# A four-layer preactivation network: the order tables of all engines are replaced

## The reference

```python
x = x + L0(_gn(x))   # three gates over (C,W), (H,C), (H,W): max and mean pool, 7x7 convolution,
                     # batch norm, sigmoid; the three are mixed by a softmax over pooled channels
x = x + L1(_gn(x))   # 3x3 convolution, 256 to 256; its weight is a softmax mix of the weight and
                     # of its circulant projections with blocks of 2, 4, 8 and 16
x = x + L2(_gn(x))   # squeeze and excitation on the mean of the wavelet's low band
x = x + L3(_gn(x))   # shifted window attention: 8x8 windows, 8 heads, bias table, mask
```

## Time and profile before

| | us |
|---|---|
| median of 3 runs | 2878.24 (2876.93 to 2885.32) |
| profiled execution | 2871.03 |
| its span, first to last instruction | 2869.2 |
| mean granted TensorE clock | 0.938 of full |
| PE busy | 2368.1 |
| DVE busy | 2303.8 |
| ACT busy | 1654.8 |
| POOL busy | 1390.7 |

### The profile page before, as it was taken

The page is one execution under the profiler, slowest core; times in us unless marked ns, Lnnn a source line. Parts: engine busy times, 40 slices in busy tenths (PEclk is TensorE's granted clock), DMA queues, the critical chain, the costliest instruction groups (busy, mean ns, idle before and its releaser), DMA issues. The chain is left out here.

```text
span 2869.2 us, 68252 instructions
## 1 busy us (share of the span) xinstructions
PE 2368.1 (83%) x27252; PEld 1337.8 (47%) x27252; DVE 2303.8 (80%) x4579; ACT 1654.8 (58%) x4200; POOL 1390.7 (48%) x1132
## 2 busy tenths in 40 slices
PE   0376828899798988899798988899798988899788
PEld 0232315444554545444554545444454545444555
DVE  7877866879888797979878797979878797978665
ACT  0322137754866568664866558664866558664665
POOL 2413561355724564355724565354824565354454
PEclk9968968999899989999899999999999999999999
DMA  5400310015010241004110241004110141001111
GB/s 147 121 1 16 122 42 24 31 38 170 16 46 23 82 133 31 31 31 148 45 46 24 76 139 32 31 31 139 55 46 24 62 145 39 31 30 45 61 52 47
DMA packets 90337, 176.13 MB, mean 61 GB/s; under 512 B 37526, under 2 KB 50470, under 8 KB 80422
## 3 DMA queue, kind: packets, MB, share of 16 engines
...
## 5 line engine op out<-in xcount | busy, mean ns | idle before, releaser
L2021 PE MATMUL F<-g_raw,cw_hi 128*128 128x512 f16 x2304 | 700.0, 386 | 28.1 <-DVE ytj L1454 10.9
L879 POOL TENSOR_TENSOR xs<-xs,rec 128x512 f32<-128x512 f32 x256 | 282.0, 1102 | 731.4 <-DVE rec L1796 728.5
L1158 ACT ACTIVATE xs<-xs,mx 128x64 f32<-128x64 f32 x1792 | 447.4, 336 | 131.4 <-DVE mx L1791 131.4
L2021 PE MATMUL F<-g_raw,cw_lo 128*128 128x512 f16 x1152 | 443.6, 385 | 0.0
L2021 PEld LDWEIGHTS F<-g_raw,cw_hi 128*128 128x128 f16 x2304 | 222.6, 99 | 296.4 <-issue 19.6
L1780 DVE TENSOR_TENSOR xs<-SP,bias 128x512 f32<-128x512 f32 (+2 forms) x384 | 181.8, 501 | 120.2 <-PE SP L2112 118.8
L864 POOL TENSOR_TENSOR tmp<-X,uw 128x512 f32<-128x512 f32 x128 | 171.5, 1351 | 179.1 <-DVE X L1636 114.3
L1795 DVE TENSOR_REDUCE sums<-xs 128x8 f32<-128x512 f32 x256 | 172.9, 675 | 95.1 <-ACT xs L1158 69.2
L2080 PE MATMUL QP<-tok_hi,qkv_hi 128*128 128x512 f16 x470 | 182.8, 389 | 51.9 <-ACT qq L1139 28.9
L1369 DVE SCALAR_TENSOR_TENSOR g_raw<-l0c,gn,g_raw 128x512 f16<-128x512 f32 x192 | 171.2, 934 | 50.0 <-ACT g_raw L1016 35.2
L2140 PE MATMUL O<-prt,vv 64*32 64x64 f32 x8192 | 175.0, 228 | 32.1 <-ACT prt L1165 28.3
...
## 6 DMA issues: line engine op xcount, KB each, us to landing
scratch_x<-X SPq DMA_DIRECT2D x32, 1024.0 KB, 7.4
...
X<-in_x SPq DMA_DIRECT2D x25, 1024.0 KB, 5.5
...
l0c<-in_x SPq DMA_DIRECT2D x7, 1024.0 KB, 5.6
...
```

The costliest lines, as they stand in the source:

```text
L879: G.tensor_tensor(keyed(sc[:, u % 4, :]), keyed(sc[:, u % 4, :]), rec[:, u % 4, :].unsqueeze(2).to_broadcast([P, 8, TOK]), ALU.mult).then_ ...
L1158: last = S.activation(keys, keys, ACT.Exp, bias=mx[:, u % 4, i:i + 1])
L2021: last = T.matmul(F[:, n % 2, :], wgt[:, ci, C3 * comp + dx, P * co:P * co + P], win[which], start=(ci == 0 and dx == 0 and j == 0), stop= ...
```

## The change

The four tables get new contents for all five engines: `FIRST`, `TURN` and `LAST_ROWS` in full, and in `AHEAD` seven entries: SP `S` 1 to 2, `Z` 2, `F` 1 and `G` 1 new; ACT `Q` 4 to 5 and `K` 1 to 2; DVE `S` 2 to 3; PE `S` 1 new. Each stream keeps its items and their order, and no other line of the program changes. Cut to what is spoken of below:

```diff
--- before.py
+++ after.py
@@ -50,96 +50,95 @@
 FIRST = {
-    "SP": {"reduce0": "Y", "reduce11": "Y", "hwgate": "Y", "band1": "Z", "band2": "YF", "hwmean3": "Z",
-        "conv10.0": "G", "conv13.0": "F", "conv14.0": "F", "conv15.0": "Z", "conv22.1": "F", "convend": "ZL"},
-    "POOL": {"load": "RR", "norm0a": "Y", "norm0b": "RY", "reduce0": "R", "reduce4": "R", "reduce5": "RR",
-        "reduce7": "R", "reduce9": "R", "reduce12": "RRRR", "reduce13": "R", "reduce14": "R", "zpool": "R",
-        "hwgate": "RRRRR", "hwrows": "R", "band0": "R", "band1": "R", "band2": "R", "band3": "R", "hwmean4": "R",
-        "hwmean5": "R", "lift2": "D", "conv0.1": "Y", "conv2.0": "D", "conv3.0": "DD", "conv7.1": "D",
-        "conv8.0": "W", "conv8.1": "D", "conv9.0": "W", "conv11.1": "WW", "conv13.1": "W", "conv14.0": "W",
-        "conv15.0": "W", "conv16.1": "W", "conv19.0": "W", "conv20.0": "W", "conv21.1": "W", "conv23.0": "WWWWW",
-        "convend": "RRRRERRRRRRRRRRRRRRERRRRRRRRRR"},
...
-    "DVE": {"load": "YYCCUCCCCCCCCCUCCUYYYYYYYYCYCYCY", "norm0a": "Y", "norm0b": "YYUU", "norm0c": "YYYYYYYYYYY",
-        "reduce1": "UU", "reduce2": "Y", "reduce3": "U", "reduce4": "UU", "reduce5": "U", "reduce6": "UU",
-        "reduce8": "U", "reduce10": "UU", "hwrows": "Y", "band0": "Y", "band1": "Y", "hwmean2": "Y",
-        "hwmean3": "Y", "logits": "Y", "mix": "Y", "mixturn": "Y", "gate12": "Y", "gate14": "Y", "gate15": "Y",
-        "norm1c": "Y", "conv1.0": "B", "conv2.0": "Y", "conv5.0": "B", "conv6.0": "B", "conv6.1": "BJ",
-        "conv7.1": "J", "conv8.1": "BJB", "conv10.0": "BBVVY", "conv11.0": "V", "conv11.1": "Y", "conv12.1": "V",
-        "conv13.0": "JVYJ", "conv13.1": "JB", "conv14.1": "B", "conv15.0": "VB", "conv15.1": "BVV",
-        "conv16.1": "BV", "conv17.0": "VYVV", "conv18.0": "VVJYJ", "conv19.1": "VC", "conv20.1": "VJCVY",
-        "conv21.0": "VCV", "conv21.1": "C", "conv22.0": "CVC", "conv22.1": "CV", "conv23.0": "V",
-        "conv23.1": "VUY", "convend": "VJJJVVVVVVVVUUUUEEUCECCUUUUEUCEUEEUUECUCEUCCC"},
-    "PE": {"reduce9": "Y", "hwgate": "Y", "hwmean4": "Y", "hwmean5": "Y", "gate12": "Y", "gate15": "Y",
-        "gate17": "Y", "conv23.1": "EEEE", "convend": "EE"},
+    "SP": {"load": "YY", "reduce1": "Y", "band2": "Z", "hwmean6": "Y", "gate9": "Z", "gate14": "F",
+        "conv0.0": "FG", "conv2.0": "Z", "conv4.0": "F", "conv7.0": "F", "conv13.0": "Z", "conv17.1": "L"},
+    "POOL": {"load": "RRRRRRRRY", "reduce0": "R", "reduce4": "Y", "reduce5": "R", "reduce9": "RR",
+        "reduce10": "RR", "reduce12": "RR", "zpool": "R", "hwconv": "R", "band1": "R", "band3": "RR",
+        "bandcopy": "RR", "hwmean1": "R", "hwmean4": "R", "hwmean6": "RR", "logits": "R", "lift2": "D",
+        "conv0.1": "D", "conv3.0": "DDD", "conv5.1": "Y", "conv7.1": "W", "conv8.0": "D", "conv9.1": "W",
+        "conv10.0": "W", "conv12.0": "W", "conv16.1": "W", "conv17.0": "W", "conv18.0": "W", "conv18.1": "W",
+        "conv19.0": "W", "conv22.0": "WWW", "conv23.1": "WWWW", "convend": "RERRRRRRRRRRRRRRRRRRERRRRRRRRR"},
...
+    "DVE": {"load": "YCYCCUUUCUCCCCUCCCCCCCCYYYYYY", "norm0a": "Y", "norm0b": "Y", "norm0c": "YYYY",
+        "reduce1": "YYY", "reduce2": "YYYYYYY", "reduce3": "YYY", "reduce4": "U", "reduce6": "YU",
+        "reduce7": "UU", "reduce8": "U", "reduce10": "U", "reduce11": "U", "reduce12": "U", "reduce13": "U",
+        "reduce14": "U", "reduce15": "U", "hwgate": "Y", "hwrows": "YYY", "band0": "Y", "logits": "Y", "mix": "Y",
+        "mixturn": "Y", "gate16": "Y", "norm1b": "Y", "norm1c": "Y", "lift0": "Y", "conv3.1": "Y",
+        "conv5.0": "BB", "conv5.1": "B", "conv6.0": "JJJB", "conv7.1": "B", "conv8.0": "V", "conv8.1": "VV",
+        "conv9.0": "B", "conv10.0": "BYV", "conv10.1": "V", "conv11.1": "BV", "conv12.1": "B",
+        "conv13.0": "JVBJVB", "conv13.1": "JB", "conv16.0": "B", "conv16.1": "YCUV", "conv17.0": "U",
+        "conv18.1": "VVYJ", "conv19.0": "YYJYCVJ", "conv20.0": "VV", "conv21.0": "UVVCC", "conv21.1": "VCVV",
+        "conv22.0": "U", "conv22.1": "V", "conv23.0": "VV", "conv23.1": "V",
+        "convend": "JYJJVVCVVVVVVVECECCECUUUUUUEUUCUEEECCECEUUCCU"},
+    "PE": {"reduce12": "Y", "reduce15": "Y", "zpool": "Y", "hwmean1": "Y", "hwmean3": "Y", "logits": "Y",
+        "conv3.0": "Y", "convend": "EEEEEE"},
 }
...
 TURN = {
-    "SP": {"reduce0": "L", "reduce3": "S", "reduce13": "L", "hwmean4": "S", "logits": "L", "gate0": "S",
-        "gate10": "L", "gate11": "SL", "gate17": "S", "lift3": "L", "conv0.0": "S", "conv1.1": "Z",
-        "conv7.0": "L", "conv7.1": "S", "conv8.1": "F", "conv15.0": "F", "conv15.1": "L", "conv16.0": "Z",
-        "conv16.1": "FZ", "conv18.1": "F", "conv21.0": "G", "conv21.1": "Z", "conv23.1": "S"},
...
-    "DVE": {"norm0a": "TE", "norm0b": "ESUUSA", "norm0c": "KKTA", "reduce0": "TU", "reduce1": "U", "reduce2": "T",
-        "reduce3": "UUU", "reduce5": "U", "reduce6": "SS", "reduce7": "U", "reduce8": "UU", "reduce9": "S",
-        "reduce10": "TT", "reduce11": "U", "reduce12": "AKA", "reduce13": "K", "reduce14": "TS", "reduce15": "U",
-        "hwgate": "T", "band0": "SST", "band2": "TKA", "band3": "K", "bandcopy": "SA", "bandturn": "T",
...
-        "conv21.1": "TVVVSCCCKVACC", "conv22.0": "U", "conv23.1": "ACK", "convend": "JJJVCVVVVVVVEETEEUESCESEC"},
-    "PE": {"norm0b": "QTQWQ", "reduce0": "Q", "reduce1": "TQ", "reduce3": "Q", "reduce4": "QT", "reduce5": "SW",
-        "reduce6": "TWQ", "reduce7": "WS", "reduce9": "Q", "reduce11": "Q", "reduce12": "TQ", "reduce13": "TW",
-        "reduce14": "Q", "reduce15": "W", "zpool": "QT", "hwconv": "QWQ", "hwrows": "TQWS", "band1": "Q",
...
-        "conv19.0": "QWSW", "conv20.1": "TQ", "conv22.0": "Q", "conv22.1": "Q", "conv23.1": "QQTWQQEE",
-        "convend": "TWEESTWEWQES"},
+    "SP": {"reduce0": "Z", "reduce2": "SF", "reduce8": "Z", "reduce10": "G", "reduce14": "L", "reduce15": "SLS",
+        "hwconv": "L", "band1": "S", "bandturn": "L", "hwmean0": "S", "gate13": "L", "gate14": "S", "lift0": "L",
+        "conv0.0": "Z", "conv6.1": "S", "conv14.1": "LS", "conv15.0": "L", "conv17.0": "F", "conv18.1": "Z",
+        "conv20.0": "FF"},
...
+    "DVE": {"norm0a": "S", "norm0b": "TESESUA", "norm0c": "KKAT", "reduce0": "TU", "reduce1": "UU",
+        "reduce3": "UU", "reduce4": "U", "reduce5": "TU", "reduce6": "SS", "reduce7": "U", "reduce8": "ST",
+        "reduce10": "U", "reduce11": "UA", "reduce12": "S", "reduce13": "AKKT", "reduce15": "TUUT",
...
+        "conv20.0": "SVTUVVVVT", "conv20.1": "CSVV", "conv21.0": "SV", "conv22.1": "CCVVCTVVUCCCKA",
+        "conv23.0": "VK", "conv23.1": "A", "convend": "JJJCVVVVVVVVEETEECECCECSCE"},
+    "PE": {"norm0a": "Q", "norm0b": "STQQ", "reduce0": "Q", "reduce1": "TQ", "reduce3": "WQ", "reduce4": "WQT",
+        "reduce5": "S", "reduce6": "WQT", "reduce7": "SW", "reduce8": "Q", "reduce11": "Q", "reduce12": "Q",
+        "reduce13": "T", "reduce14": "Q", "zpool": "TQ", "hwconv": "W", "hwgate": "TQWTQWW", "hwrows": "QS",
...
+        "conv18.1": "TWW", "conv19.1": "WS", "conv21.1": "Q", "conv22.0": "Q", "conv22.1": "Q", "conv23.0": "Q",
+        "convend": "TQQWQTEWETQTEWESEWQE"},
 }
 
-AHEAD = {"SP": {"S": 1, "L": 1}, "POOL": {"N": 5, "O": 2, "R": 28, "E": 2}, "ACT": {"X": 4, "T": 7, "Q": 4, "O": 2, "E": 1, "K": 1}, "DVE": {"S": 2, "T": 4, "A": 2, "U": 13, "E": 2}, "PE": {"Q": 3, "T": 4, "W": 4}}
+AHEAD = {"SP": {"S": 2, "L": 1, "Z": 2, "F": 1, "G": 1}, "POOL": {"N": 5, "O": 2, "R": 28, "E": 2}, "ACT": {"X": 4, "T": 7, "Q": 5, "O": 2, "E": 1, "K": 2}, "DVE": {"S": 3, "T": 4, "A": 2, "U": 13, "E": 2}, "PE": {"Q": 3, "T": 4, "W": 4, "S": 1}}
...
```

More of the change, by code:

```diff
@@ L134 @@
 LAST_ROWS = {
-    "SP": "LSLSLSLSLSLSLSLSSLS",
-    "POOL": "ENEONNNNXOXNXNXNXNNXONXNXNXXNONXNXXNXNXONXNNXXNXXNONNXXNONXNXNXXNOXNNXXNXNXOXNNNO",
-    "ACT": ("QTQTEKTXQOQXXTKKXTKQTTQQQOXKKKTKXQKXQTQQTXXKTKXOQTXQKQQXTKKKTXTOXQTKQXTQQXKTXKTOXKXTQQKQKQXTTXXT"
-           "KXTOKXKKQTQQQTTXOKKTXKQQXQTQTXKTXKOKXTXQQQQXTKXTTOXXTXTTTOK"),
-    "DVE": ("TESESTTAKAKTSPSTPSSKKAATTSTTSSKKPSPAATTTSSTKPKPTAASSTSTSTSPKPTKAASTTSSTSTSPTPKKATASSTSPPSKKATATT"
-           "SSTKPPSKAATTSTSSTSPSTPTTAAAA"),
-    "PE": ("QTQQWTQWTQWTQQWSQQSQQTQQQTQWTSQQWWTSWQQQTQTQQQQWSTWTWWTSQQQQQTQQSWTQWSTWWTQQQQQQWTSQTWSTQWWTWTQQ"
-           "QQQQTWSTWQWSQTQQQQQTWQWTQSTQWWSTQQQQQQTSQTWSWTWWTQQQTWTWTWWQQ"),
+    "SP": "SZFZLSLSLSLSLSLSLSLSSSLG",
@@ new lines @@
+    "POOL": "ENEONNNNXOXNXNNXXNNXOXNXNNXONXXXNNXNXXNONXNXNXNXXNONNXXXNONNXNXXOXNNXNXNXNXXNONNO",
+    "ACT": ("KQQTTQTEKOQXXKKQXKTKTXQQQTQTOXKKXTQKQXQQTTKXXKTOXKQTXQQXKQTKKTXTKOXKQTKQQXQXTTXKTXOXKTQKQKTQQXTX"
+           "KTXOTXKTKKXQQQTQTXKOKXXTKQTQKQXQTKTXOXKTQXQTQQXTXTXOTXKXTTKTO"),
+    "DVE": ("SETESSTKAKATTSSPTPKKTAASSTSTSTPKSSPKAATTTSSKKPPTAASSTTTSSSKTTPPKASATTSSTSSPTPTKKAATSSSTPPSKKATAT"
+           "TSSPPKSTSTKAATTSSTSSPTPTTAAAA"),
+    "PE": ("QSTQQTWQQQWTQTWSWQQSQQTQQQQWTSTQQWTWWSTQQQQQQQTQSWTWTWSWQQTQQQQWTSQTQSWTWWTQQQQTQQQSWTQSWTWWTWTQ"
```

(1 more changed line is left out.)

## The result

| | before | changed |
|---|---|---|
| median of 5 runs, us | 2879.3 (2876.9 to 2885.3) | 2863.6 (2856.2 to 2864.7) |
| profiled execution / its span, us | 2871.0 / 2869.2 | 2863.6 / 2861.8 |
| mean granted TensorE clock | 0.938 | 0.946 |

The ratio is 0.994, with a 95% interval from 0.9926 to 0.9955: 0.6% faster, some 16 us. The forecast was 37 us.

The account below looks back on a forecast made before the run. VectorE was taken to pace the head of each period and TensorE the body; -10 - 8 - 3 - 19 + 3 = -37 us on a span of 2869.2 gave 2832.2, plus 9.0 made 2841 us, range 2818 to 2882.

Parts of the forecast that it names:

- Start up to the convolution: Image 0 before its convolution: sums earlier -8 us, `Y28` +2.2, `Y31` and `Y32` -4.4; -10 us, bounds -4 and -13.
- Convolution of image 0: GpSimd's all-reduce goes behind both additions VectorE waited 13.4 us for; -8 us, bounds -4 and -8.3.
- Between image 0 and 1: VectorE's letters there change by two `C` more, three `U` fewer, one `Y47` more; -3 us, bounds -2 and -4.
- The period: Images' repeat: TensorE work moves from body to head (`convend` to next `reduce` end); -2.7 us each, -19 in seven.
- The tail: After the last convolution: TensorE gets 7.7 us more work, about 6 where VectorE leads; +3 us, bounds 0 and +8.
- SyncE at nothing: Next input's last quarter is fetched after a row store; some 8 us of cover, so costed at nothing.
- (a): Rival: body work does not pay, TensorE's waits reopen, each period costs +1.0 us; 2867 us, chance 0.18.
- (b): Rival: all the work moved out of the body pays, -31.5 us instead of -19; 2829 us, chance 0.15.
- (c): Rival: SyncE's fetch comes late and holds statistics, norm's mean and head; 2909 us, chance 0.09.
- (d): Rival: right TensorE durations change little, start's gains are lost to small waits in the periods; 2876 us, chance 0.08.

Follow-up runs that it names:

- e9: Changed kernel with three instead of nine of GpSimd's row sums `R` ahead of its first all-reduce in the first image; 2871.2 us, 0.9978 of before.
- e8: Changed kernel with GpSimd's second setup all-reduce `Y` moved back from `conv5.1` to `conv0.1` in the first image; 2868.9 us, 0.9962 of before.
- e14: e5 with GpSimd's ninth sum of the first image moved ahead of the all-reduce in the load; 2847.6 us, 0.9887 of before.
- e6: Changed kernel with the squeeze chain ahead: TensorE's third and fourth `E` and ScalarE's `E` moved earlier; 2875.3 us, 0.9981 of before.
- e5: Changed kernel with three VectorE `C` steps moved from the convolution's end to behind the first and third `E`; 2846.0 us, 0.9884 of before.
- e1: Changed kernel's table of the first image with the old tables for the other seven images; 2861.4 us, 0.9938 of before.
- e2: Old table of the first image with the changed tables of the turn, what runs ahead and the last rows; 2882.7 us, 1.0016 of before.
- e4: Changed kernel with SyncE's turn, ahead and last-rows tables as before; 2899.3 us, 1.0073 of before.

## Why the prediction was right and wrong

**Direction right, size wrong**: 16 us instead of 37. Step by step, in the order of the sum:

*Start up to the convolution, -10: right in size, wrong in one mark.* The first convolution matmul is at 217.2, 12.3 us earlier. The sums are its main term: `zpool` 9.7 us earlier where 8 was said, and e9 gives 9.3 back. I had said that `zpool` would then wait no more. It waits as before, because VectorE gained more than I gave it: TensorE's first step of `norm0a` is 15.3 us earlier, since setup steps (`Y8` to `Y12`), which I hadn't followed, went behind it. That the wait stayed means that the last sum alone sets `zpool` in both kernels.

*Convolution of image 0, -8: right.* From the first matmul to `conv23.1` it is 9.8 us shorter, and e8 shows the cause; its exact size isn't known better than the 3 us by which one and the same order differs there (e14).

*Between image 0 and 1, -3: wrong, it was +3.* I counted VectorE's letters and not those of GpSimd. VectorE's second half of the squeeze waits for GpSimd's `part`, GpSimd's second `E`, and stands behind 19 sums in the new table and 18 in the old. This wait is 9.15 us; before, it was 3.9. So GpSimd set the pace there in both kernels, and what VectorE gained by its letters only made its wait longer. The rows of both profiles take the +3 apart (before, then changed):

```profile
364.22 2.35 POOL L924 TENSOR_TENSOR tmp<-X 128x1024 f32<-128x1024 f32 x1 [0.80 <-DVE y L1653]
...
394.91 0.70 POOL L874 TENSOR_TENSOR part<-part,neg_half 128x2 f32<-128x2 f32 x1
```
```profile
344.96 2.34 POOL L923 TENSOR_TENSOR tmp<-X 128x1024 f32<-128x1024 f32 x1 [2.20 <-DMA X<-in_x]
...
376.11 0.70 POOL L873 TENSOR_TENSOR part<-part,neg_half 128x2 f32<-128x2 f32 x1
376.85 0.16 DVE L1710 SCALAR_TENSOR_TENSOR part<-F,part 128x2 f32<-128x2 f32 x1 [9.15 <-POOL part L873]
```

From the first sum to the second `E` it is 31.15 us instead of 30.69: the sum more costs 0.5. But the first sum starts 12.3 us behind the last convolution matmul (332.7) instead of 9.4 (354.8): 2.8 us. Half of that is the fetch of the next input, for which it now waits 2.2 us where it had waited 0.8 us for VectorE; the other half is that GpSimd's weighed rows ahead of it start later (5.1 against 3.7 us), as VectorE is at `conv23.0` of image 0 2.8 us behind TensorE, where it was 0.2. No run tried either by itself.

*The period, -2.7 each and -19 in all: the step that failed.* It has two faults. The first is in "the letters of TensorE change by four `Q` more ... +5.9 us of TensorE work, and as many fewer in the body". I took the letters at `convend` as the head's, as the table writes them. But TensorE has no instruction of the main line at `convend`, so the letters at `conv23.1` (`QQTWQQEE` before, none after) stand behind its last convolution matmul as well and were the head's already. Counted from that matmul to `reduce0`, TensorE has `E6 Q8 S2 T4 W5` before and `E6 Q8 S2 T5 W4` after, and up to `zpool` two `W` fewer and nothing else. The rows say the same: 848 matmuls in the head before and 783 after (a `W` has 32), and 61.6 us of TensorE in the head before, 60.2 after, and 226.5 and 226.0 in the body. Nearly nothing was moved (-1.4 us, where +5.9 was said), so nothing could be gained by it. The second fault is that I costed VectorE's letters in the head by their sum (+1.0 us) and not by what stood right ahead of the step that releases TensorE. Those are the `C` steps; placed behind the first `E` they are free, where they stood they cost some 2.3 us a period (e5, 16 us in 7).

With that one fault mended the new turn is better than the old one: e5 and e1 differ in the turn alone, and their ratios are 0.9884 and 0.9938, 15.5 us or 2.2 us for each of 7 images. The profiled periods show 1.4 us of it (325.0 against 326.4). That is near to the forecast 2.7, but by luck and not for the reason I gave, and which of the turn's other moves bring it was not tried. It isn't the stretch at the convolution's end, where e5 is still 2.0 us longer than e1 (28.1 against 26.1), nor the convolution (136.3 against mostly 135.7). It lies between `norm0a` and `conv0.0`, where e1 takes 161.3 to 165.1 us and e5 159.8 to 161.9, at clocks that differ as well. The shortest single period is even one of the old turn (322.3 us, image 6 of before and of e1; e5's shortest of these is 324.3).

*The tail, +3: right in number, by luck.* From the last convolution matmul to the end it is 219.7 us against 216.7. But the count behind it (`4 Q, 2 T, 1 W and 2 E more`, +7.7 us) has the same fault of the boundary: with the letters at `conv23.1` both kernels have `E6 Q74 S18 W40` in the tail, and the new one a single `T` more (3163 matmuls against 3159, 182.1 us of TensorE against 180.1). And e2, which has the same tail, shows no loss from image 7's first step on (520.2 us; before 520.5, the changed kernel 522.0).

*SyncE at nothing: held in the periods*, and e4 shows what it rests on. Between image 0 and 1 the changed kernel does wait for a fetch (the 2.20 us above), but by the table of the first image, which that term didn't speak of.

*The rivals.* (a), periods of +1.0 and 2867 us, is the nearest: the turn costs 0.6 us a period in e2. But its mechanism, TensorE's waits in the body opening again, isn't what happened; the body stayed as it was, and the head grew. (b) falls with its 5.9 us. (c) did not occur. (d) counted on small waits to eat the gains of the start; they didn't, e1 keeps them whole. Its observation stands, the clock being where it was: 0.90 in the head, 0.99 in the body.
